# Causal attention: the step by which scores, dots and batches are put in order, halved from two to one

## The chip, the cores and the metric

The kernel runs on one core of a Trainium2 chip. The metric is the device time of one execution in microseconds (us), as the median of several runs. Five engines work beside each other, each through its own queue in order: TensorE (PE, whose weight loads are listed apart as PEld), VectorE (DVE), ScalarE (ACT), GpSimd (POOL) and SyncE (SP, which issues DMAs). They wait for each other through semaphores. PE writes its results to PSUM buffers of 2 KB a partition, and ScalarE or VectorE reads them there.

## The reference

The input is 16 images of 56 x 56 tokens (3136) with 32 channels. The whole is a chain of a window attention, two small token MLPs, and then two layers L2 and L3, each a causal attention over all 3136 tokens of an image and an expert-choice layer. Around the causal attentions stand a residual addition and a normalisation. The change is in the causal attention, which is in short:

```
Q = embeddings @ W_Q;  K = embeddings @ W_K;  V = embeddings @ W_V
scores = einsum('bqd,bkd->bqk', Q, K) / sqrt(32)
masked = where(causal, scores, -inf)
probs = softmax(masked, axis=-1)
out = einsum('bqk,bkd->bqd', probs, V)
```

## The kernel before, in words

`causal_attention` is called once for L2 and once for L3, with all 16 images. An image has 25 tiles of 128 tokens, and its queries are cut into 7 blocks: blocks 0 to 5 of 512 queries, block 6 of the last 64. W_Q and W_K are folded into one 32 x 32 matrix, so that keys are the normalised tokens turned (`L2a_vT`, four copies on four strips of 32 partitions) and queries are these times the matrix (`L2a_qT`, "q").

Each score is computed twice, in two layouts. For the softmax's shift, "dots" put 128 queries on the partitions and up to 512 keys on the columns (L415); VectorE takes the largest of each row (L551, "max"), and when a block's are all there, one reduction gives the negated largest (L573, for block 6 L576). SyncE then writes this shift with 8 small DMAs as a row into `L2a_qT` (L283), where it rides along in the dot product. Only then can "scores" be computed for that block: keys on the partitions, 512 queries on the columns (L394). The first score of a block waits for the DMAs (L390). ScalarE takes the exponential (L514), GpSimd blanks what lies above the diagonal (L357), and a batch of up to 12 of these goes through "pv", the product with v (L487). After a block's last batch ScalarE copies the sum (L524, "acc"), PE turns it (L464, "final"), VectorE divides, and GpSimd adds it to the residual. Beside this PE turns the next image's tokens (L445, "vT") and multiplies them for q (L453), and ScalarE copies both (L536). The block on the diagonal is masked for the maxima by a product with a matrix of -1e30 (L404, "mask"), put into the same PSUM buffer as the dots of kind "edge".

Scores, dots and q use 32 of PE's 128 rows. A score uses strip 0 or 1 by the parity of its number, dots strip 2 or 3 by theirs, q strip 0. All other products use 128 rows.

Everything is put in order by one list, `WORK`. A score has its number as its time; a maximum n has the time n * NS / NM - LEAD (`max_time`), with NS = 1344 scores, NM = 1360 maxima with their masked ones and LEAD = 28, so that an image has 84 scores and 85 maxima and the maxima run 28 steps ahead. A batch has the time of its last score plus LAG = 6, and the other items are put at times beside these. The list is sorted by time divided by two in whole numbers, then by rank (score, max, q, pv, acc, final, vT, mask), then by time. Each engine walks `WORK` and issues its own part of it. PSUM gives RING = 7 buffers (`L2a_r0` to `L2a_r6`); the items that need one take them in turn in the order of `WORK` (`PLACE`), and PE waits in `bank_free` until the item seven places before has been read. A masked maximum shares the buffer of its mask. Where in a block the masked maximum stands is decided in the loop over `banks`: at the first place where its time falls one step behind a batch, so that the mask is beside the batch.

Of the kernel before, what the change touches and what calls it, by code (L numbers as in the profile page):

```python
# [71 lines left out]
def causal_attention(nc, m, k, wq, wk, wv, eps, tag):  # L72
# [60 lines left out]
    MAXES, MASK_AT = [], {}  # L133

    def max_time(n):
        return n * NS / NM - LEAD

    for img in range(NB):
        for j in range(NJ):
            banks = max_banks(j)  # L140
            spots = [(len(MAXES) + i, x[0]) for i in range(len(banks) + 1) for x in BATCHES
                     if x[0] // 2 == max_time(len(MAXES) + i) // 2 - 1]
            spot, at = spots[0] if spots else (len(MAXES), max_time(len(MAXES)) - 2)
            MASK_AT[spot] = at
            banks.insert(spot - len(MAXES), ("edge", 0))
            MAXES += [(img, j, x) for x in banks]


    RANK = {"max": 1, "score": 0, "q": 2, "pv": 3, "acc": 4, "final": 5, "vT": 6, "mask": 7, "rs": 8, "ors": 9, "res": 10, "out": 11, "vr": 12, "v": 13}
    timed = [(n, ("score", n)) for n in range(NS)]  # L150
# [3 lines left out]
    for img in range(NB):  # L154
# [4 lines left out]
        for f in range(NJ):  # L159
            at = (img - 1) * PER + (4, 12, 20, 28, 38, 48, 58)[f]  # L160
            if img == 0:
                at = min(max_time(max_at(0, f)) - 8, 2 * f - 20)
            else:
                at = min((x[0] for x in BATCHES), key=lambda t: abs(t - at))
# [3 lines left out]
        timed += [(vr - 19, ("res", img)), (vr - 7, ("rs", img)), (vr, ("vr", img)), (v, ("v", img))]  # L168
        out = (img + 1) * PER + 28
        timed += [(out, ("out", img)), (out + 14, ("ors", img))]  # L170
    WORK = [x for at, x in sorted(timed, key=lambda y: (y[0] // 2, RANK[y[1][0]], y[0]))]


    BANKED = [x for x in WORK if x[0] in ("mask", "score", "vT", "q", "final") or x[0] == "max" and x[1] not in MASK_AT]
    PLACE = {x: n for n, x in enumerate(BANKED)}
    COPIED = {x: n for n, x in enumerate(y for y in WORK if y[0] in ("vT", "q"))}
    FILLED = {x: n for n, x in enumerate(y for y in WORK if y[0] in ("vT", "q", "final"))}
    FINAL = {x: n for n, x in enumerate(y for y in WORK if y[0] == "final")}
    STAT = {x: n for n, x in enumerate(y for y in WORK if y[0] in ("res", "out"))}
    ROOT = {x: n for n, x in enumerate(y for y in WORK if y[0] in ("rs", "ors"))}  # L180
    assert [(x[0] == "res", x[1]) for x in STAT] == [(x[0] == "rs", x[1]) for x in ROOT]
# [1759 lines left out]
```

How the kernel before makes its waits and increments, by code:

```python
        @block.gpsimd  # L45
        def _(pool):
            nc.gpsimd.memset(k.ident[:], 0.0).then_inc(made, 1)
            nc.gpsimd.memset(k.mask_qk[:], 0.0).then_inc(made, 1)
            nc.gpsimd.memset(k.mask_kq[:], 0.0).then_inc(made, 1)
            nc.gpsimd.memset(k.basis[:], 0.0).then_inc(made, 1)
            pool.wait_ge(made, 4)
            nc.gpsimd.affine_select(out=k.ident[:], in_=k.ident[:], compare_op=ALU.not_equal, fill=1.0,
                                    base=0, pattern=[[-1, P]], channel_multiplier=1).then_inc(made, 1)
            nc.gpsimd.affine_select(out=k.mask_qk[:], in_=k.mask_qk[:], compare_op=ALU.is_ge, fill=NEG,
# [2 lines left out]
                                    base=-3 * P, pattern=[[1, 4 * P]], channel_multiplier=-1).then_inc(made, 1)  # L57
            nc.gpsimd.affine_select(out=k.basis[:].rearrange("p (r c) -> p r c", r=4),
                                    in_=k.basis[:].rearrange("p (r c) -> p r c", r=4),
                                    compare_op=ALU.not_equal, fill=1.0,
                                    base=0, pattern=[[0, 4], [-1, C]], channel_multiplier=1).then_inc(made, 1)
            pool.wait_ge(made, 8)
            nc.gpsimd.memset(k.basis[0:1, :], -1.0).then_inc(made, 1)
            nc.gpsimd.tensor_copy(k.ident_bf[:], k.ident[:]).then_inc(made, 1)
            pool.wait_ge(made, 10)
            nc.gpsimd.memset(k.basis[:, 0:4 * C:C], 0.0).then_inc(made, 1)
            pool.wait_ge(made, 11)
```

## Time and profile before

| | us |
|---|---|
| median of 3 runs | 4983.87 |
| lowest and highest | 4981.26, 4990.91 |
| the profiled execution | 4985.18 |
| its span | 4983.4 |
| PE busy in the span | 4412.7 (89%) |
| VectorE busy | 3200.3 (64%) |
| ScalarE busy | 2848.2 (57%) |
| GpSimd busy | 1291.6 (26%) |

The attention of L2 runs from about 1667 to 3171 us of the span, that of L3 from about 3313 to 4824. PE's busy time is modelled from pipelined matmuls, so that overlapping ones count once. A timeline merges instructions of a line that follow each other closely; each of its rows gives the start, the length, the engine, the line, the operation, the tiles and the count, and in brackets the idle time before it with what ended it.

### The profile page before, as it was taken

To read this page: it belongs to the slowest core of one execution; us is meant where nothing else is said; L and a number is where in the kernel's file an instruction comes from. 1 tells how busy PE (TensorE), PEld (TensorE's weight loads), DVE (VectorE), ACT (ScalarE), POOL (GpSimd) and SP (SyncE) were. 2 spreads that over 40 slices of the span, in tenths; PEclk is the share of its full clock that TensorE was granted. 3 is DMA by queue.
4 is the path that set the end of the run, shared out by engine and by line. 5 is a ranking of instruction groups with operands and counts; after the bars stand their busy time and mean duration, and the time that the engine had idled before them with its cause. 6 is when DMAs were issued, how large, how long until landed. Compare 5 with 4: busy or idle time off the path is not lost. (4 is left out here: it accounts for less than half of the span.)

```text
span 4983.4 us, 101485 instructions
## 1 busy us (share of the span) xinstructions
PE 4412.7 (89%) x39002; PEld 2705.1 (54%) x39002; DVE 3200.3 (64%) x6579; ACT 2848.2 (57%) x5770; POOL 1291.6 (26%) x2222
## 2 busy tenths in 40 slices
PE   4888888878688699999999999779999999999985
PEld 2666666666333355555555555455555555555544
DVE  4777777777698566666666666535666666666643
ACT  2666666666487255555555655415655556555541
POOL 3121121220000233332333431222323333334220
PEclk8989989999798699999999999869999999999987
DMA  1100000000000000000000000000000000000003
GB/s 24 31 2 2 2 2 2 2 2 2 3 1 1 1 2 2 1 2 2 2 2 2 2 2 2 5 1 2 2 2 2 2 2 2 2 2 2 2 6 52
DMA packets 348179, 22.52 MB, mean 5 GB/s; under 512 B 346388, under 2 KB 347700, under 8 KB 347700
## 3 DMA queue, kind: packets, MB, share of 16 engines
q1 hardware_dynamic: 347700, 16.03, 4.4%
q8 instruction: 313, 5.13, 0.4%
q14 instruction: 166, 1.36, 0.1%
HBM read 7.88 MB, written 6.42 MB: 3 GB/s over the span
## 5 line engine op out<-in xcount | busy, mean ns | idle before, releaser
L551 DVE TENSOR_REDUCE L3a_mx<-L3a_r 128x1 f32<-128x512 f32 (+4 forms) x1344 | 771.2, 628 | 332.8 <-PE L3a_r L415 325.2
L551 DVE TENSOR_REDUCE L2a_mx<-L2a_r 128x1 f32<-128x512 f32 (+4 forms) x1344 | 771.3, 628 | 330.4 <-PE L2a_r L415 322.7
L415 PE MATMUL L3a_r<-L3a_vT,L3a_qT 32*128 32x512 f32 (+3 forms) x3488 | 885.4, 529 | 13.3 <-DVE L3a_mx L551 12.5
L415 PE MATMUL L2a_r<-L2a_vT,L2a_qT 32*128 32x512 f32 (+3 forms) x3488 | 882.7, 527 | 13.1 <-DVE L2a_mx L551 12.5
L514 ACT ACTIVATE L3a_e<-L3a_r 128x512 f32<-128x512 f32 (+3 forms) x1344 | 669.5, 569 | 271.7 <-PE L3a_r L394 268.0
L514 ACT ACTIVATE L2a_e<-L2a_r 128x512 f32<-128x512 f32 (+3 forms) x1344 | 669.3, 569 | 265.5 <-PE L2a_r L394 261.8
L394 PE MATMUL L3a_r<-L3a_qT,L3a_vT 32*128 32x512 f32 (+4 forms) x3488 | 776.9, 514 | 3.5 <-DMA L3a_qT<-L3a_nm 3.2
L394 PE MATMUL L2a_r<-L2a_qT,L2a_vT 32*128 32x512 f32 (+4 forms) x3488 | 771.1, 511 | 3.4 <-DMA L2a_qT<-L2a_nm 3.3
L415 PEld LDWEIGHTS L3a_r<-L3a_vT,L3a_qT 32*128 32x128 f32 x3488 | 386.8, 190 | 156.6 <-DVE L3a_mx L551 90.2
L415 PEld LDWEIGHTS L2a_r<-L2a_vT,L2a_qT 32*128 32x128 f32 x3488 | 385.9, 189 | 156.5 <-DVE L2a_mx L551 89.9
L1438 POOL TENSOR_SCALAR win_xw<-win_xr,win_rs,win_sh 32x343 f32<-32x343 f32 (+7 forms) x432 | 186.9, 447 | 945.0 <-DVE win_sh L1307 944.9
L394 PEld LDWEIGHTS L3a_r<-L3a_qT,L3a_vT 32*128 32x128 f32 x3488 | 355.0, 188 | 132.0 <-issue 76.3
L394 PEld LDWEIGHTS L2a_r<-L2a_qT,L2a_vT 32*128 32x128 f32 x3488 | 352.4, 187 | 128.9 <-issue 73.5
L487 PE MATMUL L3a_acc<-L3a_e,L3a_v 128*32 128x512 f32 (+4 forms) x3680 | 356.1, 467 | 3.9 <-issue 3.0
L487 PE MATMUL L2a_acc<-L2a_e,L2a_v 128*32 128x512 f32 (+4 forms) x3680 | 356.3, 467 | 3.6 <-issue 2.7
L1082 PE MATMUL win_sl<-win_mq,win_xw 113*64 113x196 f32 x2048 | 215.8, 355 | 102.2 <-issue 65.2
L1196 ACT COPY win_mq<-win_pq 32x392 f32<-32x392 f32 x512 | 246.5, 481 | 94.5 <-PE win_pk L1075 88.6
L1235 ACT COPY win_yb<-win_yp 64x512 f32<-64x512 f32 x256 | 148.5, 580 | 206.8 <-PE win_yp L1164 205.3
L357 POOL TENSOR_SCALAR_AFFINE_SELECT L3a_e<-L3a_e 128x128 f32<-128x128 f32 (+2 forms) x304 | 99.5, 328 | 613.7 <-ACT L3a_e L514 601.5
L357 POOL TENSOR_SCALAR_AFFINE_SELECT L2a_e<-L2a_e 128x128 f32<-128x128 f32 (+2 forms) x304 | 99.4, 328 | 607.1 <-ACT L2a_e L514 594.8
L487 PEld LDWEIGHTS L2a_acc<-L2a_e,L2a_v 128*32 128x32 f32 x3680 | 119.0, 111 | 230.2 <-issue 129.4
L487 PEld LDWEIGHTS L3a_acc<-L3a_e,L3a_v 128*32 128x32 f32 x3680 | 118.2, 111 | 231.2 <-issue 130.5
(368 smaller groups left out, 7256.8 us busy)
## 6 DMA issues: line engine op xcount, KB each, us to landing
L2a_qT<-L2a_nm SPq DMA_DIRECT2D x768, 0.5 KB, 2.0
L3a_qT<-L3a_nm SPq DMA_DIRECT2D x768, 0.5 KB, 2.0
T<-in_x SPq DMA_DIRECT2D x16, 384.0 KB, 3.8
out<-T SPq DMA_DIRECT2D x16, 384.0 KB, 4.0
win_mq<-win_nmt SPq DMA_DIRECT2D x256, 3.1 KB, 1.7
win_msk<-in_L_conv_pos_emb SPq DMA_DIRECT2D x49, 0.2 KB
L2a_qT<-L2a_nm SPq DMA_DIRECT2D x32, 0.2 KB, 1.8
L3a_qT<-L3a_nm SPq DMA_DIRECT2D x32, 0.2 KB, 1.8
```

What stands on the lines that cost most here:

```text
L357: nc.gpsimd.affine_select(out=e, in_=e, compare_op=ALU.is_ge, fill=0.0, base=0, pattern=pattern, channel_multiplier=-1).then_inc(mask_done, 1)
L394: last = nc.tensor.matmul(bank_of(x)[0:r, o:o + c1 - c0], VT[g0:g0 + C, img % 2, u * P:u * P + r], QT_[g0:g0 + C, img % 2, j * QB + c0:j * ...
L415: return nc.tensor.matmul(bank_of(x)[:, o:o + c1 - c0], QT_[g0:g0 + C, img % 2, q0:q0 + P], VT[g0:g0 + C, img % 2, c0:c1], start=start, st ...
L487: last = nc.tensor.matmul(ACC[cg:cg + C, a:b], V[0:r, img % 2, u, :], E[0:r, n % RE, o + a - c0:o + b - c0], start=start, stop=stop)
L514: nc.scalar.activation(E[0:r, n % RE, 0:w], bank_of(x)[0:r, 0:w], ACT.Exp).then_inc(exp_done, 1)
L551: return nc.vector.tensor_reduce(to, frm, AX.X, ALU.max)
L1082: last = nc.tensor.matmul(bank[half * SLOT:(half + 1) * SLOT, c0:c0 + HK], window(n, 2 * p + half), buf[:, slot, half, p].rearrange("p h c ...
L1196: last = nc.scalar.copy(MQ[0:C, q_slot(n), :, :, h, :], PQ[h * C:(h + 1) * C, 0:NW * K].rearrange("p (w f c) -> p f w c", f=2, c=K))
L1235: last = nc.scalar.copy(YB[r, n % 2, :, :, half, :].rearrange("p a h c -> p (a h) c"), YP[r, :].rearrange("p (a c) -> p a c", c=C))
L1438: last = nc.gpsimd.tensor_scalar(dst, s, RS[:], SH[:], ALU.mult, ALU.add)
```

## The change

The list is sorted by the time in steps of one in place of two, and the place of the mask goes by the same step.

```
@@ -139,7 +139,7 @@
             spots = [(len(MAXES) + i, x[0]) for i in range(len(banks) + 1) for x in BATCHES
-                     if x[0] // 2 == max_time(len(MAXES) + i) // 2 - 1]
+                     if x[0] // 1 == max_time(len(MAXES) + i) // 1 - 1]
@@ -168,7 +168,7 @@
-    WORK = [x for at, x in sorted(timed, key=lambda y: (y[0] // 2, RANK[y[1][0]], y[0]))]
+    WORK = [x for at, x in sorted(timed, key=lambda y: (y[0] // 1, RANK[y[1][0]], y[0]))]
```

So two scores and two dots become one and one and again one and one. As the buffers are taken in the order of the list, what each item waits for changes too. The rows below are PE's, in the L2 attention, in program order; `L2a_r3` is buffer 3 of the ring, `L2a_exp_done` is told by ScalarE after an exponential, `L2a_max_read` by VectorE after a maximum, `L2a_item_copied` by ScalarE after a copy of vT or q, `L2a_shift_in` by the DMAs of the shift.

The first place is the middle of a run in block 4, around the q product (L453). Before:

```order
L394 MATMUL L2a_r3<-L2a_qT,L2a_vT 128x512 [waits L2a_max_read]
L394 MATMUL L2a_r4<-L2a_qT,L2a_vT 128x512 [waits L2a_max_read]
L415 MATMUL L2a_r5<-L2a_vT,L2a_qT 128x512 [waits L2a_item_copied]
L415 MATMUL L2a_r6<-L2a_vT,L2a_qT 128x512 [waits L2a_exp_done]
L453 MATMUL L2a_r0<-L2a_vT,L2a_A 128x512 [waits L2a_item_copied,L2a_exp_done]
L394 MATMUL L2a_r1<-L2a_qT,L2a_vT 128x512 [waits L2a_max_read]
L394 MATMUL L2a_r2<-L2a_qT,L2a_vT 128x512 [waits L2a_max_read]
L415 MATMUL L2a_r3<-L2a_vT,L2a_qT 128x512 [waits L2a_exp_done]
L415 MATMUL L2a_r4<-L2a_vT,L2a_qT 128x512 [waits L2a_exp_done]
```

The same place in the changed kernel:

```order
L394 MATMUL L2a_r3<-L2a_qT,L2a_vT 128x512 [waits L2a_exp_done]
L415 MATMUL L2a_r4<-L2a_vT,L2a_qT 128x512 [waits L2a_max_read]
L394 MATMUL L2a_r5<-L2a_qT,L2a_vT 128x512 [waits L2a_item_copied]
L415 MATMUL L2a_r6<-L2a_vT,L2a_qT 128x512 [waits L2a_exp_done]
L453 MATMUL L2a_r0<-L2a_vT,L2a_A 128x512 [waits L2a_item_copied,L2a_max_read]
L394 MATMUL L2a_r1<-L2a_qT,L2a_vT 128x512 [waits L2a_exp_done]
L415 MATMUL L2a_r2<-L2a_vT,L2a_qT 128x512 [waits L2a_max_read]
L394 MATMUL L2a_r3<-L2a_qT,L2a_vT 128x512 [waits L2a_exp_done]
L415 MATMUL L2a_r4<-L2a_vT,L2a_qT 128x512 [waits L2a_max_read]
```

The dots behind q waited for ScalarE's exponential of a score before, and wait for VectorE's read of a maximum now; the scores behind q the other way round.

The second place is the head of block 5, with the score that waits for the shift. Before:

```order
L404 MATMUL L2a_r1<-mask_qk,ident_bf 128x64 [waits L2a_max_read]
L394 MATMUL L2a_r2<-L2a_qT,L2a_vT 128x512 [waits L2a_exp_done]
L394 MATMUL L2a_r3<-L2a_qT,L2a_vT 128x512 [waits L2a_exp_done]
L415 MATMUL L2a_r1<-L2a_vT,L2a_qT 128x64
L415 MATMUL L2a_r4<-L2a_vT,L2a_qT 128x512 [waits L2a_max_read]
L394 MATMUL L2a_r5<-L2a_qT,L2a_vT 128x512 [waits L2a_max_read]
L394 MATMUL L2a_r6<-L2a_qT,L2a_vT 128x512 [waits L2a_shift_in,L2a_ot_ready]
L415 MATMUL L2a_r0<-L2a_vT,L2a_qT 128x512 [waits L2a_item_copied]
L415 MATMUL L2a_r1<-L2a_vT,L2a_qT 128x512 [waits L2a_max_read]
L453 MATMUL L2a_r2<-L2a_vT,L2a_A 128x512 [waits L2a_item_copied,L2a_exp_done]
L404 MATMUL L2a_r3<-mask_qk,ident_bf 128x512 [waits L2a_exp_done]
L394 MATMUL L2a_r4<-L2a_qT,L2a_vT 128x512 [waits L2a_max_read]
```

The same place in the changed kernel:

```order
L404 MATMUL L2a_r6<-mask_qk,ident_bf 128x64 [waits L2a_max_read]
L394 MATMUL L2a_r0<-L2a_qT,L2a_vT 128x512 [waits L2a_exp_done]
L415 MATMUL L2a_r6<-L2a_vT,L2a_qT 128x64
L394 MATMUL L2a_r1<-L2a_qT,L2a_vT 128x512 [waits L2a_max_read]
L415 MATMUL L2a_r2<-L2a_vT,L2a_qT 128x512 [waits L2a_exp_done]
L394 MATMUL L2a_r3<-L2a_qT,L2a_vT 128x512 [waits L2a_max_read]
L415 MATMUL L2a_r4<-L2a_vT,L2a_qT 128x512 [waits L2a_ot_ready]
L394 MATMUL L2a_r5<-L2a_qT,L2a_vT 128x512 [waits L2a_item_copied]
L415 MATMUL L2a_r6<-L2a_vT,L2a_qT 128x512 [waits L2a_max_read]
L453 MATMUL L2a_r0<-L2a_vT,L2a_A 128x512 [waits L2a_item_copied,L2a_exp_done]
L404 MATMUL L2a_r1<-mask_qk,ident_bf 128x512 [waits L2a_exp_done]
L394 MATMUL L2a_r2<-L2a_qT,L2a_vT 128x512 [waits L2a_shift_in,L2a_max_read]
```

The score with `L2a_shift_in` stood before q and the next mask (two rows further on before, the dots and then L453 and L404), and stands behind one more pair of dots, q and that mask now. One score and one maximum less stand ahead of the batch (L487) that comes before this place.

## Rows read from the trace of the kernel before

**Rows 1.** The page: busy time by engine, and the granted clock of 40 slices.

```profile
PE 4412.7 (89%) x39002; PEld 2705.1 (54%) x39002; DVE 3200.3 (64%) x6579; ACT 2848.2 (57%) x5770; POOL 1291.6 (26%) x2222
...
PEclk8989989999798699999999999869999999999987
```

**Rows 2.** Windows, one image of L2's attention: length, busy us by engine, clock, DMA.

```profile
2073.50:2165.80 92.30, 91.44 (x766) 51.94 (x765) 56.57 (x112) 53.77 (x113) 32.68 (x54) 0.98 0.05 2
```

**Rows 3.** Groups by shape, 1700 to 2300 us: count, busy us, mean ns, idle before.

```profile
L415 PE MATMUL L2a_r<-L2a_vT,L2a_qT 32*128 32x512 f32 x863 | 297.6, 646 | 0.2
...
L551 DVE TENSOR_REDUCE L2a_mx<-L2a_r 128x1 f32<-128x512 f32 x393 | 249.7, 685 | 65.5 <-PE L2a_r L415 64.8
L514 ACT ACTIVATE L2a_e<-L2a_r 128x512 f32<-128x512 f32 x422 | 224.0, 599 | 89.9 <-PE L2a_r L394 89.5
```

**Rows 4.** Waits over 14 images, 1798 to 3084 us: total us, times, longest.

```profile
DVE L2a_mx L551 <- PE L2a_r L415: 256.8, 238, 3.0
...
PEld L2a_r L394 <- issue: 62.7, 209, 2.0
...
PEld L2a_r L415 <- ACT L2a_e L514: 46.7, 112, 0.7
...
PEld L2a_r L394 <- ACT L2a_e L514: 16.5, 84, 0.2
```

**Rows 5.** Timeline of VectorE, the same image.

```profile
2111.81 1.29 DVE L551 TENSOR_REDUCE L2a_mx<-L2a_r 128x1 f32<-128x512 f32 x2 [0.33 <-PE L2a_r L415]
...
2123.57 2.48 DVE L551 TENSOR_REDUCE L2a_mx<-L2a_r 128x1 f32<-128x512 f32 x4 [2.58 <-PE L2a_r L415]
2126.45 1.89 DVE L551 TENSOR_REDUCE L2a_mx<-L2a_r 128x1 f32<-128x512 f32 x3 [0.39 <-PE L2a_r L415]
2128.37 0.18 DVE L573 TENSOR_REDUCE L2a_nm<-L2a_mx 128x4 f32<-128x28 f32 x1
...
2134.48 0.83 DVE L551 TENSOR_REDUCE L2a_mt<-L2a_r 64x1 f32<-64x64 f32 x2 [1.06 <-PE L2a_r L415]
2136.34 1.30 DVE L551 TENSOR_REDUCE L2a_mt<-L2a_r 64x1 f32<-64x512 f32 x2 [1.02 <-PE L2a_r L415]
...
2159.86 1.29 DVE L551 TENSOR_REDUCE L2a_mx<-L2a_r 128x1 f32<-128x512 f32 x2 [0.44 <-PE L2a_r L415]
...
2162.84 1.29 DVE L551 TENSOR_REDUCE L2a_mx<-L2a_r 128x1 f32<-128x512 f32 x2 [0.23 <-PE L2a_r L415]
```

**Rows 6.** Timeline of PE's weight loads, blocks 4 and 5 of this image.

```profile
2124.34 0.29 PEld L453 LDWEIGHTS L2a_r<-L2a_vT,L2a_A 32*128 32x128 f32 x2 [0.20 <-ACT L2a_e L514]
2124.88 0.33 PEld L394 LDWEIGHTS L2a_r<-L2a_qT,L2a_vT 32*128 32x128 f32 x3 [0.24 <-DVE L2a_mx L551]
2125.29 0.18 PEld L415 LDWEIGHTS L2a_r<-L2a_vT,L2a_qT 32*128 32x128 f32 x1
...
2127.01 0.29 PEld L415 LDWEIGHTS L2a_r<-L2a_vT,L2a_qT 32*128 32x128 f32 x2 [0.46 <-ACT L2a_e L514]
...
2133.24 0.19 PEld L394 LDWEIGHTS L2a_r<-L2a_qT,L2a_vT 32*128 32x128 f32 x2
...
2133.77 0.18 PEld L394 LDWEIGHTS L2a_r<-L2a_qT,L2a_vT 32*128 32x128 f32 x1 [0.22 <-issue]
...
2135.14 0.18 PEld L394 LDWEIGHTS L2a_r<-L2a_qT,L2a_vT 32*128 32x128 f32 x1 [0.75 <-issue]
...
2135.29 0.29 PEld L453 LDWEIGHTS L2a_r<-L2a_vT,L2a_A 32*128 32x128 f32 x2
2136.34 0.10 PEld L404 LDWEIGHTS L2a_r<-mask_qk,ident_bf 128*128 128x128 bf16 x1 [0.76 <-ACT L2a_e L514]
2136.66 0.19 PEld L394 LDWEIGHTS L2a_r<-L2a_qT,L2a_vT 32*128 32x128 f32 x2 [0.23 <-issue]
```

**Rows 7.** Timeline of SyncE, 2124 to 2137 us.

```profile
2128.62 4.98 SPq L283 DMA_DIRECT2D L2a_qT<-L2a_nm  x8
```

**Rows 8.** PE's wait on L390, 2130 to 2140 us: first and last start.

```profile
L390 PEldq EVENT_SEMAPHORE  x1: 51/51/51, 2135.1 to 2135.1; - x1
```

## The prediction

> **What bounds the kernel now.** I read the page first, then the windows by image, then the waits, then the timelines of single runs. The page shows PE busy for 89% of the span, and the one window of an image inside an attention layer shows 91.4 of 92.3 us, at a granted clock of 0.98, that is the 2.4 GHz level nearly throughout [rows 1, 2]. This is not PE at its peak: a dot product with 512 columns is shown for 646 ns, and four of them, on four strips of 32 rows, are in flight at once [rows 3]. In the same image VectorE is busy 56.6 us and ScalarE 53.8 us [rows 2], so over an image neither is the bound.
>
> The reader should see the image as about ten runs. In a run PE issues scores and dots for the maxima into a ring of 7 buffers; between the runs it does batches of products with v, transposes and masks, which need all 128 rows. Within a run VectorE is the slowest: a maximum over 512 columns takes 685 ns, an exponential 599 ns [rows 3], and PE could issue four dots in less time than VectorE needs for two of them. So a run costs its start (1.24 us from the loads at 2133.24 to the first maximum at 2134.48) [rows 6, 5], then one maximum after the other for as long as VectorE isn't starved, then the drain of PE. Time that VectorE idles in the middle of a run is therefore time of the kernel; its idle time between runs, which is most of the 256.8 us in the waits, is not [rows 4].
>
> Two kinds of idle time in mid-run can be read off. First, image 4 has seven gaps behind PE of 0.17 to 0.44 us, the first 0.33 at 2111.81 and the last 0.23 at 2162.84, in sum 2.06 us [rows 5]. In the order before, scores and dots come two and two, and behind each of the seven stands the first maximum of a pair. The second follows with no gap: the row at 2159.86 holds both [rows 5]. The reason is the ring. The first of a pair can be issued only after VectorE has read the buffer of the maximum three before it, and about 1.2 us pass between the load and VectorE's start (2125.29 to 2126.45) [rows 5, 6], so 1.2 us stand against two maxima of 0.685, a spare of under 0.2 us. With the q product put into the ring it is even a score's exponential that the first waits for.
>
> Second, in every image PE stops in front of the first score of query block 5. That score needs the shift row, and the chain is: the last maximum of the block ends, L573 at 2128.37 takes 0.18 us, SyncE issues 8 DMAs from 2128.62 over 4.98 us, and PE's wait on L390 ends at 2135.1 [rows 5, 7, 8]. The loads show it: at 2135.14 one goes out for that score after 0.75 idle; VectorE, which finds no work behind it, idles 1.02 us before 2136.34 [rows 5, 6]. The waits put this down to "issue" [rows 4], so the list by releaser hides it.
>
> **The change part by part.** Nothing is computed more or less; PE's, VectorE's, ScalarE's and GpSimd's queues are permuted by at most a few places, and SyncE's stays. I go by the profiled execution, 4985.2 us, span 4983.4; the median of the runs is 1.3 us lower.
>
> Shift wait. Before, one run's head holds mask, S S M M S, then the waiting score. In the new order it holds mask, S M S M S M S M, then q, then the next mask, then the waiting score. So PE does one more maximum, q and the drain and mask of the next block while the DMAs are on their way; before, it did q, the drain and the mask after the wait (loads at 2135.29 and 2136.34) [rows 6]. From the shift score to the scores behind the mask took 2135.14 to 2136.66 before [rows 6]. In the new order I get for image 4: run begins about 2132.9, q goes out about 1.6 us later (it has to wait for its buffer), 1.1 us of dots drain, mask 0.3, so the waiting score starts near 2135.85, at which time the row has landed, and the next score starts beside it. The second of the two was at 2136.66, so 0.8 us an image, for 32 images (16 in each of two layers) 26 us. Bounds: nothing, if something else holds the run at that place; 1.37 us an image (2133.77, when the score before it went out, to 2135.14) [rows 6], 44 us, if the whole wait goes.
>
> Gaps in mid-run. In the new order a maximum is no longer tied to its neighbour: each is issued at the latest when the maximum four before it is read (three with q in the ring), so three maxima, 2.05 us, stand against the 1.2 us. The gap at 2126.45 (0.39) shows it. Its dots were loaded at 2125.29, after the exponential of the score whose buffer they take; in the new order they take the buffer of a maximum that VectorE had read at 2124.9 (the second of the four from 2123.57, by 0.685 each) [rows 5, 3], and the gap goes. But a maximum now also stands behind a score whose own buffer is released by VectorE's read, and some maxima get later by that. Taking the old releases of all buffers for both orders, some two gains stand against one loss. I take 0.6 of the 2.06 us an image, 19 us in 32 images; bounds nothing and 66 us.
>
> Later scores. Every second score goes out one maximum (0.685) later. ScalarE has the room, 53.8 busy of 92.3 [rows 2], and a batch of products with v needs exponentials six scores back, so in a run that is hidden. Its cover is gone where dots take a score's buffer: those waits are 46.7 us over 14 images before the loads of L415 [rows 4], 3.3 an image. I take a tenth more of them, 0.33 an image, 10 us; bounds nothing and, if they double, 107 us.
>
> Products with v, masks and transposes: counted in PE's two orders, the changes between 32-row and 128-row work are 519 before and 521 after for a layer, at up to 0.76 us of idle loads each (2136.34) [rows 6]; two more are 3 us for both layers, inside the rest.
>
> Sum: -26 - 19 + 10 = -35, so 4985.2 - 35 = 4950, and as a median 4949.
>
> **What speaks against it.** q uses strip 0, as every second score does. In rows, q is loaded at 2124.34 and the next score, on the same strip, at 2124.88, 0.54 us later, though its buffer had been read at 2124.3 (the first of the four from 2123.57) [rows 6, 5]. The Trainium skill, page "TensorE: Matmul & The Clock Gate", section "Part 3: Packing small matmuls — row/col tiling", says that a weight load runs beside dots in flight only if it goes to another group of rows; by that, the trace agrees.
>
> **The rivals.** (a) More than forecast: all mid-run gaps and all of the shift wait go, 66 + 44 = 110 us; half way there is 4985 - 70 = 4915. For it: both lie on VectorE's chain. Against it: a few of these gaps are a tail score's 10 pieces on one strip, which stay.
>
> (b) Nothing: what VectorE gains in mid-run it waits at the run's end for PE, since the run ends with PE's drain and not with VectorE. For it: VectorE idles 2 to 3 us at each batch anyway. Against it: PE's last dots wait for buffers that VectorE frees. Time 4982, within 10 us.
>
> (c) Slower: strips. The place is q and the one or two scores beside it, and every mask that now stands after an odd number of scores. Counted in the two orders, 131 scores, dots and q of a layer had the same strip in use fewer than four places ahead of them, and 206 have in the new one. Price: 75 more conflicts a layer at up to 0.54 us, 81 us for two layers; with half of them exposed, 40, and with the gains above halved (-22) and the later scores (+10) 4985 + 28 = 5013. It decides from the point where PE, not a buffer, is late at those places; against it stands that loads in the run stand idle for a buffer again and again (0.24 behind VectorE at 2124.88, 0.46 behind ScalarE at 2127.01) [rows 6].
>
> (d) The change doesn't do what it says: excluded, PE's order shows it everywhere but for the first 28 steps, which have maxima alone.
>
> **How the numbers follow.** Forecast, -10 to -60 us: 0.54. (a): 0.12. (b): 0.17. (c): 0.17. A measurement of this kernel tells about 0.2% (10 us) from no change. Faster: forecast and (a), and a little of (b): 0.67. Same: 0.15. Slower: 0.18. The forecast's own range is 4925 to 4975. For 8 in 10 it goes down to 4908 (most of (a)) and up to 5003 (all of (b) and half of (c)).
>
> **What would show it.** In the profile after: the 1.02 us in front of the maximum behind block 5's first score should be below 0.3; PE's "issue" idle of up to 2.0 us before L394 should be gone; the 256.8 us of VectorE over 14 images should fall by 10 to 20, and an image should take 91.2 in place of 92.3 us. VectorE, ScalarE and PE keep their busy times. Wrong would be: the shift wait there with the same length (then SyncE's DMAs got later too); loads of L394 idle longer behind ScalarE or VectorE than the 16.5 us, with no less before L415 (then the wait has only changed sides); VectorE's idle time before runs longer by what was won in them (that is (b)); or dots behind q starting half a microsecond late with their buffers free (that is (c)).

## The result, and the profile after

The changed kernel is slower: 4994.2 us median of 20 runs, against 4982.4 us of the kernel before on the same chip; ratio 1.0028, 95% interval 1.0018 to 1.0039. That is 12 us more by the medians and 14 by the ratio, where 35 us less was forecast.

The page and the granted clock of the changed kernel (profiled execution: span 4996.2 us, before 4983.4) answer to [rows 1].

```profile
PE 4434.1 (89%) x39002; PEld 2786.9 (56%) x39002; DVE 3196.9 (64%) x6579; ACT 2849.7 (57%) x5770; POOL 1288.1 (26%) x2222
...
PEclk9989989989798699999999999869999999999987
```

Three windows of the changed kernel (columns as in [rows 2]): a stretch with a low clock, the image around it, and an undisturbed image.

```profile
2168.70:2175.50 6.80, 6.80 (x26) 1.10 (x25) 1.02 (x2) 0.10 (x1) 0.23 (x1) 0.50 0.03 0
2081.69:2175.90 94.21, 93.44 (x763) 54.25 (x762) 56.46 (x112) 53.79 (x113) 32.57 (x54) 0.96 0.05 2
2638.68:2729.56 90.88, 90.11 (x763) 53.91 (x762) 56.46 (x112) 53.79 (x113) 32.58 (x54) 1.00 0.05 2
```

The kernel before has such a stretch too, in the image of [rows 2], but shorter and at another place: behind the output batch of block 0.

```profile
2084.40:2087.60 3.20, 3.20 (x30) 2.12 (x30) 0.34 (x2) 1.58 (x5) 0.25 (x1) 0.50 0.12 6
```

PE does the same 39002 matmuls and is busy 21 us longer, its weight loads 82 us; the other engines are within 4 us of before. A clock of 0.50 is the 1.2 GHz level. So there are two questions: what an image costs at 2.4 GHz, and how often the clock falls.

The waits of the changed kernel over the same stretch, 1798 to 3084 us, answer to [rows 4].

```profile
DVE L2a_mx L551 <- PE L2a_r L415: 282.3, 223, 6.1
...
PEld L2a_r L394 <- issue: 55.8, 222, 0.6
PEld L2a_r L415 <- ACT L2a_e L514: 39.9, 84, 0.6
PEld L2a_r L394 <- DVE L2a_mx L551: 35.8, 70, 1.5
...
PEld L2a_r L394 <- ACT L2a_e L514: 6.1, 28, 0.2
```

The "issue" wait of up to 2.0 us is gone (longest now 0.6), as foretold. But VectorE's wait for PE rose from 256.8 to 282.3 us where a fall by 10 to 20 was forecast (8 of these 25 us are in every image: VectorE waits 20.5 us in an undisturbed one before and 21.1 after; the rest is waited in images with a low clock), and a wait of 1.5 us behind VectorE stands in its place.

The order lays an image out around ten output batches. I name a batch by its first score, counted within the image, and read from the trace the time from one batch's first weight load to the next's; "stretch 36" is the one from batch 36 to batch 45. In images without a low clock and without a late shift these agree within 0.1 us. Both kernels do the same work in each row of this table (in the neighbouring single stretches a dot moves across a batch, so they are added up):

| from batch to batch | before | after | difference |
|---|---|---|---|
| 78 (over 0) to 3, the head | 11.86 | 11.04 | -0.82 |
| 3 to 21 | 21.00 | 21.02 | +0.02 |
| 21 to 28 | 8.00 | 7.66 | -0.34 |
| 28 to 55, block 5's head in it | 30.30 | 30.86 | +0.56 |
| 55 to 66, the tail scores in it | 12.46 | 13.36 | +0.90 |
| 66 to 78 | 6.98 | 6.94 | -0.04 |
| image | 90.60 | 90.88 | +0.28 |

In images 1 to 14 of the two layers, 28 in all, this is 8 us. The clock adds to it. In the same images the records of the granted clock show 18 stretches at 1.2 GHz before, of 3.4 us each, 17 of them at batch 0; an image with one takes 92.1 in place of 90.6 us, so 27 us in all. After, there are 19, all near the tail scores, six of them 6.8 us long; images take 92.5 or 94.2 in place of 90.9, so 13 x 1.6 + 6 x 3.3 = 41 us, 14 more. Then there are images in which SyncE's shift lands late. Before, each 0.1 us by which the wait on L390 ends later makes stretch 36 0.1 us longer, and it takes up to 13.0 us at 2.4 GHz (14.2 with a low clock in it) in place of 11.7. After, it takes 12.2 us whether the shift is late or not, and 12.4 at most, so that 7 us of before are missing (the low clock apart). Of the +12.8 us between the two profiled executions the rest is about 4 us more before the first score of the two layers, 2 us ahead of them and 8 us less in the last images. 8, 14, -7, 6 and -8 make 13.

### The profile page after: what moved, and what is told of

It reads as the page before. It is cut to its first block and busy times, and to the rows that moved or that the text cites. A ratio compares the mean times of both kernels' runs of the same rounds, so it can differ in the third digit from the quotient of the medians.

```text
span 4996.2 us, 101515 instructions
## 1 busy us (share of the span) xinstructions
PE 4434.1 (89%) x39002; PEld 2786.9 (56%) x39002; DVE 3196.9 (64%) x6579; ACT 2849.7 (57%) x5770; POOL 1288.1 (26%) x2222
## 5 line engine op out<-in xcount | busy, mean ns | idle before, releaser
L415 PE MATMUL L2a_r<-L2a_vT,L2a_qT 32*128 32x512 f32 (+2 forms) x3488 | 916.1, 523 | 0.0
L415 PE MATMUL L3a_r<-L3a_vT,L3a_qT 32*128 32x512 f32 (+2 forms) x3488 | 915.6, 523 | 0.0
L394 PE MATMUL L3a_r<-L3a_qT,L3a_vT 32*128 32x512 f32 (+4 forms) x3488 | 828.4, 507 | 12.2 <-DVE L3a_mx L551 11.5
L394 PE MATMUL L2a_r<-L2a_qT,L2a_vT 32*128 32x512 f32 (+4 forms) x3488 | 827.3, 507 | 12.1 <-DVE L2a_mx L551 11.5
L394 PEld LDWEIGHTS L3a_r<-L3a_qT,L3a_vT 32*128 32x128 f32 x3488 | 422.3, 184 | 142.7 <-issue 65.0
L394 PEld LDWEIGHTS L2a_r<-L2a_qT,L2a_vT 32*128 32x128 f32 x3488 | 421.6, 184 | 142.2 <-issue 65.0
L415 PEld LDWEIGHTS L3a_r<-L3a_vT,L3a_qT 32*128 32x128 f32 x3488 | 429.5, 188 | 94.6 <-ACT L3a_e L514 44.3
L415 PEld LDWEIGHTS L2a_r<-L2a_vT,L2a_qT 32*128 32x128 f32 x3488 | 428.6, 188 | 95.1 <-ACT L2a_e L514 44.3
L487 PE MATMUL L2a_acc<-L2a_e,L2a_v 128*32 128x512 f32 (+4 forms) x3680 | 370.0, 486 | 3.5 <-issue 2.6
L487 PE MATMUL L3a_acc<-L3a_e,L3a_v 128*32 128x512 f32 (+4 forms) x3680 | 365.6, 480 | 3.8 <-issue 2.9
L487 PEld LDWEIGHTS L2a_acc<-L2a_e,L2a_v 128*32 128x32 f32 x3680 | 119.1, 113 | 246.1 <-issue 134.9
L487 PEld LDWEIGHTS L3a_acc<-L3a_e,L3a_v 128*32 128x32 f32 x3680 | 118.3, 112 | 242.1 <-issue 129.3
```

The lines of the kernel that those rows point to most:

```text
L394: last = nc.tensor.matmul(bank_of(x)[0:r, o:o + c1 - c0], VT[g0:g0 + C, img % 2, u * P:u * P + r], QT_[g0:g0 + C, img % 2, j * QB + c0:j * ...
L415: return nc.tensor.matmul(bank_of(x)[:, o:o + c1 - c0], QT_[g0:g0 + C, img % 2, q0:q0 + P], VT[g0:g0 + C, img % 2, c0:c1], start=start, st ...
L487: last = nc.tensor.matmul(ACC[cg:cg + C, a:b], V[0:r, img % 2, u, :], E[0:r, n % RE, o + a - c0:o + b - c0], start=start, stop=stop)
```

## Where block 5's head lost what the shift gave

Weight loads and then VectorE in image 10 of the changed kernel, around the place that [rows 5, 6] show for before.

```profile
2697.93 0.10 PEld L404 LDWEIGHTS L2a_r<-mask_qk,ident_bf 128*128 128x128 bf16 x1 [0.76 <-ACT L2a_e L514]
2698.25 0.18 PEld L394 LDWEIGHTS L2a_r<-L2a_qT,L2a_vT 32*128 32x128 f32 x1 [0.23 <-issue]
...
2699.34 0.29 PEld L415 LDWEIGHTS L2a_r<-L2a_vT,L2a_qT 32*128 32x128 f32 x2
2701.12 0.18 PEld L394 LDWEIGHTS L2a_r<-L2a_qT,L2a_vT 32*128 32x128 f32 x1 [1.49 <-DVE L2a_mx L551]
```

```profile
2696.27 0.83 DVE L551 TENSOR_REDUCE L2a_mt<-L2a_r 64x1 f32<-64x64 f32 x2 [1.01 <-PE L2a_r L415]
...
2699.45 0.70 DVE L551 TENSOR_REDUCE L2a_mt<-L2a_r 64x1 f32<-64x512 f32 x1 [1.02 <-PE L2a_r L415]
2700.18 0.16 DVE L576 TENSOR_REDUCE L2a_nm<-L2a_mt 64x1 f32<-64x7 f32 x1
2700.37 1.68 DVE L551 TENSOR_REDUCE L2a_mx<-L2a_r 128x4 f32<-128x512 f32 x4
```

PE's wait on L390 now ends at 2697.4, before the first score of block 5 goes out (2698.25): nothing waits for the shift any more. But that score goes out late all the same. In us behind the first load of batch 36, in images without a late shift (before and changed are measured, the forecast follows from the prediction's times):

| | before | forecast | changed |
|---|---|---|---|
| first score of block 5 | 6.1 | 6.8 | 7.4 |
| mask | 7.3 | 6.5 | 7.1 |
| scores behind the mask | 7.6 | 6.8 | 7.4 |
| VectorE starts on the edge bank | 9.0 | - | 9.5 |
| batch 45 | 11.7 | - | 12.2 |

The scores that the run goes on with are 0.25 us earlier, not 0.8: the forecast had q at 5.5 and it is loaded at 6.0, and it let the run begin 0.3 us too early. VectorE idles the same 1.02 us, one maximum later, behind the mask. And the mask (L404) now stands in front of a score, a tail dot, a score and then the edge bank. A mask takes its buffer of the ring when it is issued, but the buffer comes free only when VectorE has read the edge bank: that read is the first of the four from 2700.37 and ends near 2701.1. Scores and dots are issued in order, and the one whose turn it is for that buffer stands 1.49 us.

## The same mechanism in the head, with the other sign

Weight loads of the kernel before in the head of image 7:

```profile
2358.53 0.18 PEld L394 LDWEIGHTS L2a_r<-L2a_qT,L2a_vT 32*128 32x128 f32 x1
2360.05 0.18 PEld L415 LDWEIGHTS L2a_r<-L2a_vT,L2a_qT 32*128 32x128 f32 x1 [1.33 <-DVE L2a_mx L551]
...
2361.17 0.81 PEld L487 LDWEIGHTS L2a_acc<-L2a_e,L2a_v 128*32 128x32 f32 x20 [0.76 <-issue]
```

and of the changed kernel in the head of image 10:

```profile
2646.07 0.18 PEld L394 LDWEIGHTS L2a_r<-L2a_qT,L2a_vT 32*128 32x128 f32 x1 [0.24 <-issue]
2646.08 0.18 PEld L415 LDWEIGHTS L2a_r<-L2a_vT,L2a_qT 32*128 32x128 f32 x1
2646.80 0.81 PEld L487 LDWEIGHTS L2a_acc<-L2a_e,L2a_v 128*32 128x32 f32 x20 [0.54 <-issue]
...
2648.04 0.10 PEld L404 LDWEIGHTS L2a_r<-mask_qk,ident_bf 128*128 128x128 bf16 x1
```

Before, the mask is issued ahead of four scores, and the last dot of the run waits 1.33 us for its buffer; then comes batch 0. In the changed order the mask falls behind batch 0 and the edge bank is read soon after it. There is no stall, and the head is 0.8 us shorter.

## The experiments

All are kernels in which the step is one or two by place. A phase is a score's number modulo the 84 of an image; `ONES` lists the phases with the step of one. With `ONES = []` this is the kernel before, with `[(0, 84)]` the changed one:

```diff
+    def step_of(t):
+        return 1 if any(a <= t % PER < b for a, b in ONES) else 2
+    def slot(t):
+        return t // step_of(t) * step_of(t)
-                     if x[0] // 2 == max_time(len(MAXES) + i) // 2 - 1]
+                     if slot(x[0]) + step_of(x[0]) == slot(max_time(len(MAXES) + i))]
-    ... key=lambda y: (y[0] // 2, RANK[y[1][0]], y[0])
+    ... key=lambda y: (slot(y[0]), RANK[y[1][0]], y[0])
```

Ratios are against the kernel before, with 95% intervals. Stretches and low stretches (those at 1.2 GHz) are read in images 1 to 14 of both layers of one profiled execution of each kernel; the executions of one kernel lie up to 38 us apart, so a few low stretches more or less show nothing. Lines from the order on stand 8 lines lower in the experiments' profiles than in those of the two kernels (14 in experiments 8 and 10, and 11 from the output batch on in 13 and 14).

**1. The changed kernel, tail scores two and two.**

```diff
-    ONES = [(0, 84)]
+    ONES = [(0, 78)]
```

> The changed kernel, but the last six score products of an image (those of block 6, phases 78 to 83 of the period) keep the step of two. Theory A (the six tail scores, each of ten passes on one strip of TensorE, no longer overlap when dots stand between them; the stretch from the batch behind score 55 to the batch behind score 66 went from 12.46 to 13.36 us): that stretch is back at about 12.5 us, 0.9 us x 32 images = 29 us less than the changed kernel, and the stretches of lower granted clock leave the end of the image. Time 4960 to 4972 us, ratio to before 0.996 to 0.998. Theory B (the loss is spread over every place where a score stands beside dots on its strip): only 6 of 84 scores are changed, so about 1 us less, 4993 us, ratio 1.0026. Theory C (only the clock): the stretch stays at 13.4 us, and the time falls by the 14 us that the low clock cost more than before, to 4980 us.

4970.4 us, ratio 0.9985 (0.9974 to 0.9997). Theory A, though smaller than it said: stretch 55 takes 12.8 us, so 0.5 of the 0.9 us comes back, and 10 low stretches stay (3 in the first layer, 7 in the second). B and C are out.

**2. The changed kernel, mask of block 5's head one step later.**

```diff
-            ... else (len(MAXES), max_time(len(MAXES)) - 2)
+            ... else (len(MAXES), max_time(len(MAXES)) - 1)
```

> The changed kernel, but the mask whose batch finds no slot in the list stands one score later (ahead of the score and the edge bank's product, no longer two steps ahead). Theory A (this mask takes the ring's bank early, its product is read late, and score 898 of image 10 stands from 2699.34 to 2701.12 us for it): the stretch from the batch behind score 36 to that behind score 45 goes from 12.2 back to 11.7 us, 0.5 x 32 = 16 us less: 4978 us, ratio to before 0.999. Theory B (the loss is spread over the image's scores): no change from the changed kernel, ratio 1.003.

4992.5 us, ratio 1.0037 (1.0023 to 1.0051): no gain. The stretch did go from 12.2 to 11.7 us, as foretold, and undisturbed images from 90.9 to 90.4. The edit also puts the first score of block 5 and the last tail dot ahead of the mask again, and with the early mask's stall its cover is gone: stretch 36 again takes up to 12.7 us where the shift lands late, 8 us over the 28 images. 24 of the 28 images have a low stretch, where 19 had one, but fewer of them are long: 88 us at 1.2 GHz in all against 85. So of 15 us won in the order 8 go to late shifts and 2 to the clock. One image, and the low stretch at the end of another:

```profile
2255.00:2347.00 92.00, 91.55 (x761) 53.92 (x760) 55.76 (x111) 53.78 (x111) 32.35 (x53) 0.98 0.05 2
1886.10:1889.40 3.30, 3.30 (x14) 0.59 (x16) 0.69 (x1) 0.00 (x0) 0.07 (x1) 0.50 0.05 0
```

An image of 90.4 + 1.6 = 92.0 us. The profiled execution is 6 us shorter than that of the changed kernel; the ratios (1.0037 against 1.0028) show no gain, and where the rest went in the other runs is open. What the mask's place costs is shown by the stretch, not by the time.

**3. Both edits.** `ONES = [(0, 78)]` and `- 1`.

> Both edits of the two kernels above together. Theory A: the two losses stand at different places of the image and add: 0.9 + 0.5 = 1.4 us x 32 = 45 us less than the changed kernel, about 4950 to 4960 us, ratio to before 0.993 to 0.996. Theory B (spread loss): about 4992 us, ratio 1.002. If one loss only hides the other (the bank or the buffer that was late is late again at the next batch), the sum is no more than that of the larger alone.

4955.6 us, ratio 0.9965 (0.9953 to 0.9978). Theory A: undisturbed images take 89.8 us, 1.04 less than in the changed kernel, which is 0.52 + 0.52 of experiments 1 and 2, and 11 low stretches are left.

**4. The kernel before, phases 6 to 41 one by one.**

```diff
-    ONES = []
+    ONES = [(6, 42)]
```

> The kernel before, but phases 6 to 41 of each period (the scores of blocks 2 and 3, and the head of block 4) take the step of one. Theory A (step one gains where the traces showed 0.3 us less in the stretch behind score 21, and loses only at the head of block 5 and in the tail scores): 0.3 to 0.6 us less per image, 4963 to 4973 us, ratio to before 0.996 to 0.998. Theory B (spread loss of 0.27 us per image, strips in conflict everywhere): 36 of 84 scores changed, about +4 us, ratio 1.001.

4914.6 us, ratio 0.9879 (0.9866 to 0.9893): 60 us less, far more than any theory gave. Stretch by stretch, the head is 0.8 us shorter and stretch 21 is 0.3 shorter; I had left the head out of the account because phase 6 seemed to lie behind it. And there is no stretch at 1.2 GHz in any of the 28 images. 1.1 x 31 + 27 = 61 us.

**5. Phases 6 to 9 alone.** `ONES = [(6, 10)]`

> The kernel before, with the step of one at phases 6 to 9 of each period alone (the four scores on either side of the output batch of block 0). There the mask of the next block moves from ahead of four scores to behind the output batch. Theory A (the edge bank that this mask holds is what the maximum after it waits for: PE stands from 2358.6 to 2360.05 us in image 7 of before, the low granted clock begins right behind, and both go): the two stretches behind the batches at phases 78 and 0 together take 11.0 in place of 11.9 us, 0.9 x 31 = 28 us less, and the 18 stretches at 1.2 GHz at 1.5 us each go as well, 27 us: 4921 us, ratio to before 0.989. Theory B (the order gains the 28 us, the clock falls elsewhere): 4948 us, 0.9945. Theory C (the gain of 61 us of the run with phases 6 to 41 is spread over its 36 scores): 4 of 36, 7 us less, 0.9985.

4928.5 us, ratio 0.9894 (0.9877 to 0.9912). Theory A: 0.82 x 31 + 27 = 52 us, and 53 are measured. The head takes 11.0 us, all other stretches are those of before, and the clock stays up over 14 images of each layer:

```profile
1798.00:3084.00 1286.00, 1282.13 (x10922) 733.13 (x10920) 807.35 (x1601) 767.25 (x1597) 446.72 (x754) 1.00 0.05 2
3446.00:4732.00 1286.00, 1282.12 (x10862) 731.54 (x10862) 811.22 (x1606) 767.35 (x1596) 452.40 (x762) 1.00 0.05 2
```

**6. Phases 12 to 41 alone.** `ONES = [(12, 42)]`

> The kernel before, with the step of one at phases 12 to 41 alone (blocks 1 to 3). Theory A: only the stretch behind score 21 gains, 0.3 us x 32 = 10 us; the stretches at 1.2 GHz behind the batch of block 0 stay: 4966 us, ratio 0.998. Theory C (gain spread evenly over the scores of phases 6 to 41): 30 of 36 parts of 61 us, 51 us less: 0.990. The forecast's own term for the gaps inside the runs (0.6 us an image) gives 19 us for the whole image and 7 us for these 30 scores: 0.9986.

4966.8 us, ratio 0.9964 (0.9950 to 0.9978). Theory A for the order: stretch 21 gives 0.3 us, 10 us in all, the rest nothing. Where the mid-run gaps were to be won, this is what they bring. The other 8 of the 18 us fit the clock: 8 low stretches in place of 18 in the profiled execution, which was the fastest of its 12 runs. Why there are fewer is open.

**7. The tail scores alone.** `ONES = [(78, 84)]`

> The kernel before, with the step of one for the six tail scores alone (phases 78 to 83). Theory A (ten passes on one strip overlap only with a score beside it): the stretch behind score 55 goes from 12.5 to 13.4 us, 0.9 x 31 = 28 us more: about 5004 us, ratio to before 1.006, and more, up to 1.009, if stretches at 1.2 GHz come up at the end of the image too. Theory D (the tail scores lose only behind a block 5 in steps of one): no change, 1.000.

5016.8 us, ratio 1.0066 (1.0046 to 1.0086). Theory A in sign, but the size is put together otherwise: stretch 55 goes to 13.1, +0.7 us, and there are 23 low stretches, 18 near the tail scores and 5 at the head, with 102 us at 1.2 GHz against 61 before. D is out.

**8. The kernel before, only the first score of block 5 three operations later.**

```diff
+    for img in range(NB - 1):
+        late = ("score", score_at(img, 5))
+        i = WORK.index(late)
+        j = next(n for n in range(i, len(WORK)) if WORK[n][0] == "mask")
+        WORK.insert(j, late)
+        del WORK[i]
```

> The kernel before with its step of two, but the first score of block 5, which waits for SyncE's shift of the maxima, stands three operations later: behind the two dots and q, right ahead of the next mask (in the last image it stays). That takes away the wait of 0.75 to 1.0 us and nothing else. The forecast priced it at 0.8 us an image: 25 us less, 4951 us, ratio 0.995. Theory A (the time comes back at the next bank, as VectorE and the edge bank behind the mask set the pace): 0 to 0.3 us an image, 4966 to 4976 us, ratio 0.998 to 1.000.

4970.0 us, ratio 0.9979 (0.9966 to 0.9992). Theory A in size: stretch 36 goes from 11.75 to 11.6 us, 5 us in all. But the edit doesn't take the wait away. Weight loads and VectorE, in the image whose batch 36 starts at 2120.28:

```profile
2126.01 0.48 PEld L467 LDWEIGHTS L2a_r<-L2a_vT,L2a_A 32*128 32x128 f32 x2 [0.35 <-DVE L2a_mt L565]
2126.38 0.29 PEld L408 LDWEIGHTS L2a_r<-L2a_qT,L2a_vT 32*128 32x128 f32 x2
2127.43 0.10 PEld L418 LDWEIGHTS L2a_r<-mask_qk,ident_bf 128*128 128x128 bf16 x1 [0.76 <-ACT L2a_e L528]
```

```profile
2125.72 2.12 DVE L565 TENSOR_REDUCE L2a_mt<-L2a_r 64x1 f32<-64x64 f32 x4 [1.06 <-PE L2a_r L429]
2127.88 0.16 DVE L590 TENSOR_REDUCE L2a_nm<-L2a_mt 64x1 f32<-64x7 f32 x1
2129.12 1.35 DVE L565 TENSOR_REDUCE L2a_mx<-L2a_r 128x4 f32<-128x512 f32 x3 [1.08 <-PE L2a_r L429]
```

The waiting score goes out at 6.1 us behind batch 36, as before, and where the shift lands late stretch 36 is still longer by as much (up to 12.6 us at 2.4 GHz). What the edit does is to fill the wait with the dots and q. VectorE's 1.02 us in front of the tail maxima are gone and stand in front of the edge bank as 1.08. The mask, behind the waiting score in both, comes at 7.15 in place of 7.30 us, the edge bank's maximum at 8.84 in place of 8.99, the batch at 11.6. So the chain is shift, waiting score, mask, edge bank. The 0.15 us are what the dots and q between the waiting score and the mask were worth; what the wait is worth the experiment doesn't tell. The other half of the gain is that 10 low stretches stood in the profiled execution in place of 18; whether that comes from this edit is open.

**9. Phases 6 and 7 alone.** `ONES = [(6, 8)]`

> The kernel before, with the step of one at phases 6 and 7 alone. Here too the mask moves behind the output batch of block 0, but there one score and one dot fewer stand in turn (S dot S dot S S dot dot q, batch, mask, S S edge). Theory M (the place of the mask is what the head gains from, not the turns): the stretches behind the batches at phases 78 and 0 sum to 11.0 to 11.3 us against 11.9 of before, no stretch at 1.2 GHz at the batch of block 0, time 4926 to 4940 us, ratio to before 0.989 to 0.992. Theory T (the turns of one give it): half of the gain of the kernel with phases 6 to 9, about 4955 us, 0.995.

4925.2 us, ratio 0.9895 (0.9877 to 0.9913), head 11.0 us, no low stretch. Theory M: the place of the mask gives the head's gain, not the turns. Its loads ahead of batch 0 (L423 and L495 are the L415 and L487 of before):

```profile
2343.09 0.29 PEld L423 LDWEIGHTS L2a_r<-L2a_vT,L2a_qT 32*128 32x128 f32 x2 [0.21 <-ACT L2a_e L522]
2343.23 0.29 PEld L461 LDWEIGHTS L2a_r<-L2a_vT,L2a_A 32*128 32x128 f32 x2
2344.28 0.81 PEld L495 LDWEIGHTS L2a_acc<-L2a_e,L2a_v 128*32 128x32 f32 x20 [0.76 <-ACT L2a_e L522]
```

The 1.33 us in front of the last dot are 0.21.

**10. The parts that gained, together.** `ONES = [(6, 42)]` and the edit of experiment 8.

> The parts that gained together: the step of one at phases 6 to 41, the step of two elsewhere, and the first score of block 5 three operations later. Theory A (the terms stand in different stretches and add, no stretch at 1.2 GHz is left to win): 0.9 + 0.3 + 0.15 us an image and the low clock gone: an undisturbed image of 89.35 us, 5 us less than the 4914.6 us of the run with phases 6 to 41, so about 4910 us, ratio to before 0.987. If the shift's wait hid behind something that the other edits took away, the forecast's 0.8 us an image shows up only here: 4890 us, 0.983.

4911.5 us, ratio 0.9869 (0.9850 to 0.9889), the fastest of all, though not told apart from experiment 4. Undisturbed images take 89.3 us, and two have a low stretch, in places where the shift lands late. The terms add. The forecast's 0.8 us for the shift does not show up, but here too the mask comes behind the waiting score.

**11. The changed kernel, only the last two tail scores as a pair.** `ONES = [(0, 82)]`

> The changed kernel, with the step of two for the last two of the six tail scores only (the last ten-pass score and the one-pass score, then their two dots side by side). In the traces the first four tail scores took 3.33 us in turns of one against 2.85 in pairs, the last two with their dots 2.92 against 2.42. Theory E (dots on strips 2 and 3 run side by side only without a ten-pass score between them, at every pair alike): 0.5 of the 0.9 us comes back, the stretch behind score 55 takes 12.9 to 13.0 us, 16 us less than the changed kernel: 4978 us, ratio to before 0.9995. Theory L (the loss sits in the first four, and the last two only follow): the stretch stays at 13.3 us, 4992 us, 1.0025.

4979.6 us, ratio 1.0004 (0.9992 to 1.0016). Theory E on time; stretch 55 takes 12.8 us, the same as with all six in pairs. So the loss sits at the last pair, and not at every pair alike. (Experiment 1, with the same stretches, is 9 us faster by the ratio: its profiled execution has 10 low stretches and this one's 18.) Loads there, in the kernel before and in the changed one:

```profile
2985.97 1.33 PEld L394 LDWEIGHTS L2a_r<-L2a_qT,L2a_vT 32*128 32x128 f32 x13
2987.37 0.30 PEld L415 LDWEIGHTS L2a_r<-L2a_vT,L2a_qT 32*128 32x128 f32 x4
2988.43 0.16 PEld L487 LDWEIGHTS L2a_acc<-L2a_e,L2a_v 128*32 128x32 f32 x8 [0.76 <-ACT L2a_e L514]
```

```profile
2724.17 0.18 PEld L415 LDWEIGHTS L2a_r<-L2a_vT,L2a_qT 32*128 32x128 f32 x1
...
2724.34 0.30 PEld L394 LDWEIGHTS L2a_r<-L2a_qT,L2a_vT 32*128 32x128 f32 x2
2725.22 0.19 PEld L394 LDWEIGHTS L2a_r<-L2a_qT,L2a_vT 32*64 32x64 f32 x2 [0.59 <-issue]
2725.48 0.29 PEld L415 LDWEIGHTS L2a_r<-L2a_vT,L2a_qT 32*128 32x128 f32 x2
2726.53 0.16 PEld L487 LDWEIGHTS L2a_acc<-L2a_e,L2a_v 128*32 128x32 f32 x8 [0.76 <-ACT L2a_e L514]
```

Before, both last dots are loaded from 2987.37 and run side by side; the batch comes 1.06 us later. In the changed order the first goes out at 2724.17 and the second at 2725.48, behind the one-pass score, which waits 0.59 for nothing that the profile names. The batch comes 2.36 us after the first dot. What holds that last score is open.

**12. Phases 42 to 77 alone.** `ONES = [(42, 78)]`

> The kernel before, with the step of one at phases 42 to 77 alone (the end of block 4 and block 5). Theory A (the early mask in front of a dot, a score and the edge bank costs 0.5 us, the dots beside it 0.1): the three stretches behind scores 28, 36 and 45 sum to 30.9 us against 30.3, 0.6 x 31 = 19 us more: 5000 us, ratio to before 1.004; the stretches at 1.2 GHz at the batch of block 0 stay or move with the longer image. The forecast (shift wait gone at 0.8, gaps in the runs gone): 35 to 40 us less, 4945 us, 0.992.

5005.6 us, ratio 1.0062 (1.0044 to 1.0080). The forecast's 4945 is out. From 28 to 55 the time is 30.9 as foretold, and stretch 55 takes 12.84 in place of 12.46, which I had booked wholly to the tail. With experiments 1 and 11 this splits the table's +0.90 into 0.38 for block 5's turns and 0.52 for the last pair (0.68 where the tail alone is changed, experiment 7). 0.56 + 0.38 us an image are 29 us. The profiled execution also has hardly a late shift that shows, as in the changed kernel (7 us less), and 88 us at 1.2 GHz in place of 61 (some 13 more); that makes 35, and it took 36 us longer than that of before (31 by the ratio).

**13 and 14. The stall put back, at the head and at block 2.** Both are the kernel of experiment 5 with, in PE's output batch (`j == 2` in the second):

```diff
+                        if j == 0:
+                            held = [y[1] for y in WORK[:WORK.index(x)] if y[0] == "max"]
+                            pe.wait_ge(max_read, held[-1] + 1)
```

> The kernel with the step of one at phases 6 to 9 (4928.5 us, no stretch at 1.2 GHz in the images), in which TensorE is made to stand again: ahead of the output batch of block 0 it waits until VectorE has read the last maximum before it, about 1.5 us after its last matmul, in a place where the kernel before stood 1.4 us for the edge bank. Theory I (this idle time next to short, half-idle runs is what the clock falls behind): stretches at 1.2 GHz are back in half of the images at that batch, so 1.4 us x 31 = 43 us for the wait and some 27 us for the clock: 4998 us, ratio to before 1.003. Theory O (the clock fell for another reason, the masks or the turns): only the wait's 43 us or less (work behind it may catch up), 4950 to 4972 us, ratio 0.994 to 0.998, and no stretch at 1.2 GHz.

> The same kernel with the same hold at another place: ahead of the output batch of block 2, where TensorE comes from a long run of scores and dots. The wait is again about 1.5 us an image, 43 to 48 us in all. Theory I in its strong form (any such idle time brings the clock down): stretches at 1.2 GHz at that batch too, 27 us more, 4998 us, ratio 1.003. Theory P (only idle time in the head, where the 15 us around it hold little work, does it): no stretch at 1.2 GHz, 4972 to 4976 us, ratio 0.999.

5011.8 us, ratio 1.0063 (1.0040 to 1.0085), and 4999.1 us, ratio 1.0031 (1.0017 to 1.0045). Theory I in both. The load of the held batch at the head, the low stretch behind it, and the two images, with and without one:

```profile
2077.23 0.84 PEld L498 LDWEIGHTS L2a_acc<-L2a_e,L2a_v 128*32 128x32 f32 x20 [2.13 <-ACT L2a_e L525]
```

```profile
2078.40:2091.90 13.50, 13.50 (x58) 6.42 (x58) 5.09 (x9) 5.24 (x12) 1.24 (x4) 0.50 0.04 2
2067.48:2164.93 97.45, 95.85 (x764) 54.08 (x763) 56.85 (x112) 53.93 (x113) 32.60 (x54) 0.93 0.04 2
2164.93:2256.74 91.81, 89.89 (x764) 51.32 (x763) 56.57 (x112) 53.82 (x113) 32.60 (x54) 1.00 0.05 2
```

The hold costs 1.6 us an image (91.4 against 89.8 us). Behind it come 6 stretches at 1.2 GHz, fewer than theory I's half of the images, but four of them are 13.7 us long and cost 6 us each. At block 2 the hold costs 1.6 us too, and there are 9 around the batch, of 3.4 us, at 1.7 us each:

```profile
1821.90:1825.20 3.30, 3.30 (x24) 1.47 (x15) 0.00 (x0) 0.00 (x0) 0.00 (x0) 0.50 0.12 6
```

Experiment 5 has none at either place. The mean granted clock, which every run has, agrees: 0.934 to 0.935 in the runs of experiment 5, 0.926 to 0.931 in 13 and 0.930 to 0.934 in 14. So a stall of PE is enough to bring the clock down at its end or right behind it, in the head and after a dense run alike, in some of the images. Which images, and why they are fewer at the head than in the kernel before (6 against 17) and longer, is open.

## Why the prediction was wrong

**The step that failed first: pricing the shift wait at 0.8 us an image, -26 us.** The wait goes, and PE's "issue" of 2.0 us with it. But the price was read from the start of one score, which the working put at 6.8 us behind batch 36. It goes out at 7.4, against 7.6 for its neighbour before, so 0.25 us were won at that place; and a run's length is not read from its start. Stretch 36 even became 0.5 us longer, because the mask that now goes ahead of that score holds its buffer until an edge bank that comes 0.5 us later. From batch 28 to 55 the change costs 0.56 us an image. What the new place does give is that a late shift costs nothing, 7 us, and this is seen only together with the early mask: with the mask behind the score again the late shifts are back (experiment 2). No run has the score behind the mask without the early mask, so its price alone stays open; experiment 8 prices only the dots and q.

**The step that was missing: where the masks fall.** The working had a line for them ("inside the rest") and counted them as changes between 32-row and 128-row work. Their real weight is the buffer that a mask holds until the edge bank is read. Block 5's mask moved ahead of the waiting score and a dot: +0.5 us an image (experiments 2 and 3), of which the late shifts that its stall hides give half back. The head's mask moved behind the batch: -0.8 us (5 and 9). The order rows of the change showed the first of them, and I read them only for q and the waiting score. The piece for the head stood in none of the places I looked at.

**The tail scores.** They were named only as gaps that stay. They cost 0.5 to 0.7 us an image (1, 7, 11), 17 to 22 us.

**Gaps in mid-run, -19 us.** In phases 12 to 41 0.3 us an image is won, 11 us (6), and block 5's turns lose 0.4 in stretch 55 (12), so that nothing is left over the image. The working took 0.685 us for each maximum, but in a row VectorE starts one every 0.6 (four in 2.48 us, [rows 5]), so three of them cover 1.8 us and not 2.05. Whether what is won is waited for later in the run was not measured.

**Later scores, +10 us.** Not seen: PE's waits of dots for ScalarE fell from 46.7 to 39.9 us over 14 images, where a rise to 51 was forecast.

**The clock.** It was not a term at all. I read 0.98 in the window as "nearly throughout" and went on. The missing 0.02 was one stretch of 3.4 us in two of three images, 27 us in all, nearly all of it behind a stall that the change removes; the change took those away and brought 41 us of others.

**Rival (c)** had the right sign for another reason. It laid the loss to strips at q and the scores beside it. From batch 3 to 21, with three q products, both kernels take 21.0 us. That the weight load beside q waits for its strip may hold, as it begins at 2124.88 together with q's second pass; but the profile lays its idle 0.24 us to VectorE, whose second read of the four from 2123.57 ends at the same time, so the row alone doesn't tell the two apart, and it costs nothing there. **Rival (b)**, gains coming back as VectorE's waits at the run's end, is the nearest to the whole picture at 2.4 GHz, but its reason was not tested: an image is the same within 0.3 us, and VectorE waits 0.6 us more in it, as large local gains and losses cancel.

## What to carry to other kernels

A change of the order moves every item, so price it by place: cut the period at fixed marks, and ask of each item that holds a buffer (here a mask that holds one until a later read) how many others now stand between its issue and its release. A wait is worth what comes earlier behind it at the end of the stretch, not what one item's start shows: follow the chain from what is waited for to that end, and see which of its links the new order leaves where they were. A stall can also hide another delay (here the late shift), so that taking it out gives less than its length. And a window's clock of 0.98 is to be resolved into its stretches before anything is summed, since a stall of 1.3 us can cost as much again in clock as in time.

## What was not expected of the hardware

- Taking away a stall of 1.33 us an image kept TensorE at 2.4 GHz through 28 images where 18 had a stretch at 1.2 GHz (experiments 4, 5 and 9; the mean granted clock is 0.934 to 0.937 in all their 16 runs, and 0.926 to 0.933 in the runs of the kernel before beside them), and putting one of 1.6 us back brought such stretches back right behind it, with lengths of 3.4, 6.8 or 13.7 us (13, 14). One outside these places fits it too: the low stretch in stretch 36 before stands behind an idle of 1.63 us in front of the score that a late shift held. The Trainium skill, page "TensorE: Matmul & The Clock Gate", section "A second HAM failure mode: psum-queue depth-cycling", tells of a kernel whose engine idles shortly between groups of matmuls and whose clock goes up and down for it. By that, these runs agree: the idles here are of 1.3 to 2.1 us.
- It is not the whole rule. The changed kernel stalls 1.49 us in block 5 and has no low stretch there in any image. Its low stretches are near the tail scores, where PE's loads show no idle time over 0.84 us, which is found in other stretches too; with the stall in block 5 taken out they stayed (24 in place of 19 in experiment 2, 88 in place of 85 us; 11 in place of 10 from experiment 1 to 3). In experiments 8 and 10 three low stretches stand in images with a late shift behind idles of only 0.9 us. What sets these is open.
- The stall of 1.49 us cost 0.5 us an image and hid another delay. With it (the changed kernel, 1, 11 and 12) late shifts lengthen stretch 36 by less than 1 us in all over 28 images; without it (before, 2 to 10, 13 and 14) by 7 to 10 us, a low stretch behind one or two of them counted in.
